# Four layers of cross-attention and FFN on one core: in the first FFN the rounding's constants move to ScalarE, the additions come one pair later, and the first products run three pairs ahead of the turned values

## The reference

```python
def fp4_quant_dequant(x):
    xb = x.reshape(shape[:-1] + (shape[-1] // 16, 16))
    scale = max(max(abs(xb)) / 6, 1e-12)
    xn = xb / scale
    idx = jnp.searchsorted(_MID, jnp.abs(xn))     # nearest of 0, .5, 1, 1.5, 2, 3, 4, 6
    return _GRID[idx] * jnp.sign(xn) * scale

h = silu(fp4_linear(x, w_gate)) * fp4_linear(x, w_up)   # 352 hidden values
x = x + tanh(g_ffn[0]) * fp4_linear(h, w_down)
```

## Time and profile before

| what | value |
|---|---|
| three runs | 792.27, 794.93, 795.2 us; median 794.93 |
| the profiled execution | 798.6 us, span from its first to its last instruction 796.8 us |
| mean granted TensorE clock | 0.897 |
| busy TensorE, VectorE, ScalarE, GpSimd | 629.9, 530.2, 325.5, 280.0 us |
| DMA | 67.73 MB, mean 85 GB/s |

### The profile page before, as it was taken

The page is one execution under the profiler, slowest core; times in us unless marked ns, Lnnn a source line. Parts: engine busy times, 40 slices in busy tenths (PEclk is TensorE's granted clock), DMA queues, the critical chain, the costliest instruction groups (busy, mean ns, idle before and its releaser), DMA issues.

```text
span 796.8 us, 10173 instructions
## 1 busy us (share of the span) xinstructions
PE 629.9 (79%) x3016; PEld 390.6 (49%) x3016; DVE 530.2 (67%) x1380; ACT 325.5 (41%) x627; POOL 280.0 (35%) x562
## 2 busy tenths in 40 slices
PE   4767876647899999898688771387887889999997
PEld 3433433334765564564334330143443666777885
DVE  8684646998762553378526647763558887998664
ACT  3142564223324334264153440315445455555553
POOL 5342354301240312115340721303123454546453
PEclk9795998777899999799899995579889999999999
DMA  8864421002204323002354330224400233444442
GB/s 260 185 172 129 86 59 55 2 0 67 66 24 135 94 42 89 8 17 77 106 147 145 58 79 0 66 70 109 136 5 1 81 90 104 119 103 110 117 120 67
DMA packets 67990, 67.73 MB, mean 85 GB/s; under 512 B 25119, under 2 KB 48223, under 8 KB 67552
## 3 DMA queue, kind: packets, MB, share of 16 engines
q1 hardware_dynamic: 61326, 64.61, 30.2%
q10 hardware_dynamic: 6610, 2.47, 1.3%
HBM read 50.29 MB, written 17.60 MB: 85 GB/s over the span
## 4 chain that ended last, share of the span: by engine, by line
PE 35%; DVE 22%; POOL 13%; issue 12%; DMA 9%; ACT 4%; SPq 4%; POOLq 0%; ACTq 0%; DVEq 0%
POOL sg L722 10%; PE ps L1803 7%; PE ps L1743 5%; PE ps L1783 5%; DVE mraw L1361 3%; DMA QG<-q_parts 3%; DMA q_parts<-loT 2%; PE ps L1705 2%; PE ps L1969 2%; SPq L330 2%; PE ps L1960 1%; PE ps L1722 1%; PE ps L1688 1%; PE ps L1694 1%; PE ps L1787 1%
## 5 line engine op out<-in xcount | busy, mean ns | idle before, releaser
L814 ACT ACTIVATE PT<-ps 110x512 f32<-110x512 f32 x192 | 111.0, 595 | 140.1 <-PE ps L1783 67.1
L1361 DVE TENSOR_REDUCE mraw<-ps 128x4 f32<-128x308 f32 x256 | 116.0, 475 | 76.8 <-PE ps L1743 31.5
L1743 PE MATMUL ps<-KG,QG 98*128 98x308 f32 x256 | 105.6, 430 | 46.3 <-DVE mraw L1361 25.8
L722 POOL TENSOR_TENSOR sg<-sg,cb 128x512 f32<-128x512 f32 x64 | 85.7, 1341 | 76.0 <-ACT sg L987 75.1
L1783 PE MATMUL ps<-QG,KG 128*110 128x512 f32 x192 | 90.9, 492 | 13.4 <-ACT PT L814 11.0
L1743 PEld LDWEIGHTS ps<-KG,QG 98*128 98x128 f32 x256 | 51.8, 206 | 89.4 <-DVE mraw L1361 60.6
L588 POOL TENSOR_TENSOR nt<-nhv,rs 128x4 f32<-128x4 f32 (+1 forms) x81 | 17.7, 218 | 165.8 <-DVE rs L1103 133.9
L1803 PE MATMUL ps<-PT,VN 128*18 128x512 f32 x512 | 72.2, 637 | 0.0
L1590 DVE TENSOR_TENSOR ps<-ps,sg 128x512 f32<-128x512 f32 x72 | 50.3, 698 | 32.3 <-POOL sg L722 29.3
L1783 PEld LDWEIGHTS ps<-QG,KG 128*110 128x110 f32 x192 | 33.9, 180 | 56.6 <-ACT PT L814 42.5
L987 ACT ACTIVATE sg<-ps 128x512 f32<-128x512 f32 x72 | 43.1, 599 | 42.6 <-PE ps L2031 42.2
(11 more groups left out here) (308 smaller groups left out, 1433.2 us busy)
## 6 DMA issues: line engine op xcount, KB each, us to landing
cb<-c_parts SPq DMA_DIRECT2D x64, 256.0 KB, 3.3
QG<-q_parts SPq DMA_DIRECT2D x48, 256.0 KB, 4.0
KG<-k_parts SPq DMA_DIRECT2D x48, 154.0 KB, 3.0
q_parts<-hiT SPq DMA_DIRECT2D x14, 256.0 KB, 2.0
q_parts<-loT SPq DMA_DIRECT2D x14, 256.0 KB, 2.0
k_parts<-kmH SPq DMA_DIRECT2D x16, 154.0 KB, 2.3
k_parts<-kmL SPq DMA_DIRECT2D x16, 154.0 KB, 2.8
VN<-v_parts SPq DMA_DIRECT2D x16, 144.0 KB, 2.8
```

Source lines behind the costliest of these rows:

```text
L722: pool.tensor_tensor(sg[:, n % 3, :], sg[:, n % 3, :], cb[:, k % CRING, :], ALU.mult).then_inc(sc_done, 1)
L814: act.activation(PT[0:w, q % PTR, :], ps[0:w, 4 + q % 2, :], ACT.Exp, scale=SCALE[l]).then_inc(exp_done, 1)
L1361: dve.tensor_reduce(mraw[:, n % 2, i, g * HG:(g + 1) * HG], ps[:, u % 2, 0:GK].rearrange("p (h k) -> p h k", k=K), AX_X, ALU.max).then_inc ...
L1743: ins = pe.matmul(o, QG[0:KS, n % 3, g, q], KG[0:KS, n % 3, g, :], start=True, stop=l not in (1, 2))
```

## The change

- VectorE's rounding is cut into `scaled(j)` (scales, product with the inverse scale, exponent bits) and `rounded(j)` (addition and subtraction). `scaled(j)` follows `product(j)`, `rounded(j-1)` follows `scaled(j)`.
- The constant (maximum with 1, times 1.5 * 2^22) is made by ScalarE in two linked instructions on 704 columns, `steps(j)`: a Relu with scale and bias, and an addition. Their biases lie in a new tile `magic`, set by two memsets.
- The factor 1 - 2^-22 on the inverse scale goes into the product as a scalar_tensor_tensor, here and in `quantise_batch`.
- `hscale` has three slots.
- TensorE: `turn(2j-6)` follows `up(2j)`, `turn(2j-5)` follows `up(2j+1)`, `down` of both behind, and only then the transposes of input 2 or 3 and of layer-1 inputs. The last four tiles' turns and downs stand between layer 1's score units 1 and 8.
- ScalarE's queue follows; `residual(0)` and `residual(1)` come after `product(4)` and `product(6)` instead of after pairs 3 and 5.

```diff
@@ -162,7 +162,8 @@
...
         qs2 = sb("qs2", [P, 2, 2, 32])
-        hscale = sb("hscale", [P, 2, 44])
+        hscale = sb("hscale", [P, 3, 44])
+        magic = sb("magic", [P, 2])
         am = sb("am", [P, 16])
@@ -279,6 +280,7 @@
...
         z_scales, z_scaled, z_steps = sem("z_scales"), sem("z_scaled"), sem("z_steps")
+        h_bits, h_steps = sem("h_bits"), sem("h_steps")
         am_w_part, am_w_ps, am_w_all = sem("am_w_part"), sem("am_w_ps"), sem("am_w_all")
@@ -640,7 +642,7 @@
...
                 pool.wait_ge(hq_scaled, j + 1)
-                pool.tensor_tensor(h, v, hscale[:, j % 2, :].unsqueeze(2).to_broadcast([P, 44, 16]),
+                pool.tensor_tensor(h, v, hscale[:, j % 3, :].unsqueeze(2).to_broadcast([P, 44, 16]),
                                    ALU.mult).then_inc(hq_done, 1)
@@ -856,6 +858,8 @@
...
                             silu(c // 3 + 1)
+                        if k == B and l == 0 and c == 6:
+                            steps(0)
                         if c == 5 and 1 <= k <= last:
@@ -886,29 +890,43 @@
...
+            def steps(j):
+
+                w = qh[:, j % 2, 1, :]
+                act.wait_ge(h_bits, j + 1)
+                act.activation(w, w, ACT.Relu, bias=magic[:, 0:1], scale=1.5 * 2.0 ** 22).then_inc(h_steps, 1)
+                act.wait_ge(h_steps, 2 * j + 1)
+                act.activation(w, w, ACT.Identity, bias=magic[:, 1:2]).then_inc(h_steps, 1)
+
             def ffn0(xT_one, q_one):
...
                 xqT_out(1)
-                for j in range(2, T // 2 + 2):
+                for j in range(2, T // 2):
+                    if j == 5:
+                        normalise_out((2, 0))
+                    for h in range(2):
+                        silu(2 * j + h)
+                        if j >= 3:
+                            hT_out(2 * j - 6 + h)
+                    if j == 7:
+                        normalise_out((2, 1))
                     if j in (3, 5):
...
                     if j in (5, 7):
-                        normalise_out((2, j // 2 - 2))
-                    if j < T // 2:
-                        silu(2 * j)
-                        silu(2 * j + 1)
+                        xT_one(j // 2 - 2)
+                    steps(j - 1)
+                    if j in (5, 7):
+                        q_one(j // 2 - 2)
                     if j == 3:
                         normalise_out((1, B - 1))
-                    if j in (5, 7):
-                        xT_one(j // 2 - 2)
-                    if j >= 2:
-                        hT_out(2 * j - 4)
-                        if j in (5, 7):
-                            q_one(j // 2 - 2)
-                        hT_out(2 * j - 3)
+                hT_out(T - 6)
+                hT_out(T - 5)
+                steps(T // 2 - 1)
+                for i in range(T - 4, T):
+                    hT_out(i)
                 normalise_out((2, 2))
@@ -1010,9 +1028,10 @@
...
+
             def quant_steps(w, src, inv):
-                link(dve.tensor_tensor(w[0], src, inv, ALU.mult))
+                link(dve.scalar_tensor_tensor(out=w[0], in0=src, scalar=1.0 - 2.0 ** -22, in1=inv, op0=ALU.mult, op1=ALU.mult))
                 link(dve.tensor_scalar(w[1].bitcast(I32), w[0].bitcast(I32), EXP_BITS, None, ALU.bitwise_and))
@@ -1142,7 +1161,8 @@
...
                 link(dve.tensor_reduce(s[0], v, AX_X, ALU.max, apply_absolute_value=True))
-                link(quant_scales(s[0], s[1]))
+                link(dve.tensor_scalar(s[0], s[0], 1.0 / 6.0, 1e-12, ALU.mult, ALU.max))
+                link(dve.reciprocal(s[1], s[0]))
                 link(quant_steps(w, v, s[1].unsqueeze(2).to_broadcast([P, 32, 16])))
@@ -1320,17 +1340,29 @@
...
                 dve.wait_ge(h_done, j + 1)
+                if j >= 3:
+                    dve.wait_ge(hq_done, j - 2)
+                link(dve.tensor_reduce(hscale[:, j % 3, :], h.rearrange("p t (n e) -> p (t n) e", e=16), AX_X, ALU.max,
+                                       apply_absolute_value=True))
+
+            def scaled(j):
+
+                v = fh[:, j % 3, :, :].rearrange("p t (n e) -> p (t n) e", e=16)
+                w = [qh[:, j % 2, i, :].rearrange("p (b e) -> p b e", e=16) for i in range(2)]
+                s = hscale[:, j % 3, :]
+                link(dve.tensor_scalar(s, s, 1.0 / 6.0, 1e-12, ALU.mult, ALU.max))
+                link(dve.reciprocal(qs[:, 1, :], s))
                 if j >= 2:
                     dve.wait_ge(hq_done, j - 1)
-                link(dve.tensor_reduce(hscale[:, j % 2, :], h.rearrange("p t (n e) -> p (t n) e", e=16), AX_X, ALU.max,
-                                       apply_absolute_value=True))
+                link(dve.scalar_tensor_tensor(out=w[0], in0=v, scalar=1.0 - 2.0 ** -22, in1=qs[:, 1, :].unsqueeze(2).to_broadcast([P, 44, 16]),
+                                              op0=ALU.mult, op1=ALU.mult))
+                dve.tensor_scalar(w[1].bitcast(I32), w[0].bitcast(I32), EXP_BITS, None, ALU.bitwise_and).then_inc(h_bits, 1)
             def rounded(j):
-
-                v = fh[:, j % 3, :, :].rearrange("p t (n e) -> p (t n) e", e=16)
-                w = [qh[:, j % 2, i, :].rearrange("p (b e) -> p b e", e=16) for i in range(2)]
-                link(quant_scales(hscale[:, j % 2, :], qs[:, 1, :]))
-                quant_steps(w, v, qs[:, 1, :].unsqueeze(2).to_broadcast([P, 44, 16])).then_inc(hq_scaled, 1)
+                w = [qh[:, j % 2, i, :] for i in range(2)]
+                dve.wait_ge(h_steps, 2 * j + 2)
+                link(dve.tensor_tensor(w[0], w[0], w[1], ALU.add))
+                dve.tensor_tensor(w[0], w[0], w[1], ALU.subtract).then_inc(hq_scaled, 1)
                 dve.wait_ge(hq_scaled, j + 1)
@@ -1401,8 +1433,10 @@
...
                     if c == 3 and l == 0 and k == B:
+                        link(dve.memset(magic[:, 0:1], -1.5 * 2.0 ** 22))
+                        link(dve.memset(magic[:, 1:2], 1.5 * 2.0 ** 22))
                         product(0)
-                        rounded(0)
+                        scaled(0)
                     if c == 9 and k == 0 and l == 0:
@@ -1475,17 +1509,18 @@
...
                     product(j)
+                    if j in (4, 6):
+                        residual(j // 2 - 2)
                     if j == 1:
...
                         quantise_batch(3)
-                    rounded(j)
-                    if j == 3:
-                        residual(0)
+                    scaled(j)
+                    rounded(j - 1)
                     if j == 5:
                         q_rest(0)
-                        residual(1)
                 q_rest(1)
+                rounded(T // 2 - 1)
                 for u in range(4 * TPB):
@@ -1923,29 +1958,42 @@
...
                 input_transposed(1)
-                for j in range(2, T // 2 + 2):
+                for j in range(2, T // 2):
+                    for h in range(2):
+                        up(2 * j + h)
+                        if j >= 3:
+                            turn(2 * j - 6 + h)
+                    if j >= 3:
+                        down(2 * j - 6)
+                        down(2 * j - 5)
                     if j in (3, 5):
                         input_transposed((j + 1) // 2)
-                    if j < T // 2:
-                        up(2 * j)
-                        up(2 * j + 1)
+                    if j == 5:
+                        pe.wait_ge(xqT_ready, B)
                     if j in (5, 7):
                         turn_input(j // 2 - 2)
-                    if j == T // 2 + 1:
-                        pe.wait_ge(silu_done, T)
-                        for u in range(2 * TPB):
-                            scores(0, u // G, u % G)
-                    if j >= 2:
-                        turn(2 * j - 4)
-                        if j >= 3:
-                            down(2 * j - 5)
-                        if j in (5, 7):
-                            queries(j // 2 - 2)
-                        turn(2 * j - 3)
-                        down(2 * j - 4)
-                down(T - 1)
-                for u in range(2 * TPB, 4 * TPB):
+                        queries(j // 2 - 2)
+                turn(T - 6)
+                turn(T - 5)
+                down(T - 6)
+                down(T - 5)
+
+                pe.wait_ge(silu_done, T)
+                for u in range(4 * TPB):
                     scores(0, u // G, u % G)
+                    if u == 1:
+                        turn(T - 4)
+                        turn(T - 3)
+                        down(T - 4)
+                    if u == 2:
+                        down(T - 3)
+                    if u == 4:
+                        turn(T - 2)
+                    if u == 6:
+                        turn(T - 1)
+                        down(T - 2)
+                    if u == 8:
+                        down(T - 1)
```

## The result

| | before | changed |
|---|---|---|
| median, first comparison (4 runs each) | 794.62 us | 784.15 us |
| ratio with its 95% interval | | 0.9864 [0.9838, 0.9891] |
| profiled execution, span | 798.6, 796.8 us | 782.29, 780.4 us |
| mean granted clock | 0.897 | 0.910 |

The change is worth 1.1 to 1.6%. Two later comparisons of the same kernel gave 0.9889 [0.9832, 0.9946] and 0.9867 [0.9843, 0.9892].

The account below looks back on a forecast made before the run. VectorE was taken to bound the kernel up to layer 1's first maxima, then TensorE's scores. VectorE's -8.4 and +3.1 made 5.3 us earlier; TensorE's scores left -5.0, so 794.93 - 5.0 = 789.9 us, range 786 to 797.

Parts of the forecast that it names:

- What VectorE saves: VectorE up to layer 1's first maxima: constant moved to ScalarE, factor folded, a wait and a slowed residual gone; -8.4 us.
- The -1.3 for product(5): VectorE's 1.28 us wait before product(5) goes, because the transposes of input 3 now stand behind pair 5's first products.
- What the new order adds: Four new VectorE waits, at batch 3's projection, product(3), rounded(2) and product(4): +1.0, +0.65, +0.3, +1.15, sum +3.1 us.
- Behind it TensorE decides: Layer 1's first scores: TensorE limits, score unit 2 comes only 3.8 us earlier; gain between 3.8 and near 8 us.
- I take a third of the way: -5.0: Score phase of layer 1: gain set a third of the way from 3.8 to near 8 us, so -5.0 us.
- B: Rival, layer 1's scores: all turns and downs disappear between scores and the clock rises early; -8, 787 us; chance 0.13.
- The rule against the change: Skill page keeps max, add, mul on VectorE; by it the move costs 9.9 us against 4.5 gained; not followed.
- the 4.5 booked: Gain booked for moving the maximum-and-scale from VectorE to ScalarE in the pairs: 8 x 0.56 = 4.5 us.
- C: Rival, inside the pairs: TensorE replaces VectorE as limit, bursts staying low; 4 us given back, 794 us; chance 0.26.
- D: Rival, layer 1's first 26 score units: clock stays low as turns and downs tear scores apart; +6, 801 us; chance 0.08.
- E: Rival, ScalarE in the pairs: Relu isn't in Silu's table, so each pair loads two tables; 795 us; chance 0.06.

## Why the prediction was wrong, point by point

- **What VectorE saves** held. L1017 and L1025 are gone at their sizes, the scalar_tensor_tensor costs 0 more (891 against 893 ns), no wait stands before product(5), and the residual of batch 3 takes 0.75 instead of 1.25 us. The -1.3 for product(5) rested on one profile: the wait was 1.28 us there and 0.60, 0.95 and 1.22 in three other executions. Missed: that contact with GpSimd wasn't removed but moved. The addition at 196.17 took 0.62 us more beside the multiplication from 195.55 to 196.94.
- **What the new order adds** held in sum, and in the first profile in place: 1.07 for 1.0 at the projection, 1.39 for 0.65 at product(3), 0.14 for 0.3 at rounded(2), 1.26 for 1.15 at product(4): 3.9 for 3.1. In the other two profiles it was 1.49 and 1.48 at the projection, 0.35 and 0.55 at product(3), 0.69 and 0.88 at product(4), and 1.02 and 1.13 at product(6), where the prediction saw 0.5 us to spare: 3.6 and 4.0 in all. Product starts relative to product(0) were 8.2, 19.1, 26.2, 33.4, 49.0, 55.4 and 65.7 us, laid out as 8.3, 19.3, 25.85, 33.2, 48.9, 55.4 and 65.9. With the slowed addition the first maximum came 74.6 behind, not 74.25; against the earlier trace rows that is 4.9 us earlier for 5.3, in the means 4.2. Part of the agreement is luck, for a gain was missing from the sum. The late addition doesn't depend on the operation ahead of it and starts 0.44 us behind that one's start; in the kernel before it did, and started 0.56 behind. First the changed kernel, then the kernel before:

```profile
140.86 0.53 DVE L1359 TENSOR_SCALAR qh<-qh 128x704 int32<-128x704 int32 x1
141.30 0.89 DVE L1364 TENSOR_TENSOR qh<-qh 128x704 f32<-128x704 f32 x1
```

```profile
205.47 0.53 DVE L1017 TENSOR_SCALAR qh<-qh 128x704 f32<-128x704 f32 x1
206.03 0.89 DVE L1018 TENSOR_TENSOR qh<-qh 128x704 f32<-128x704 f32 x1
```

Seven times 0.12 are 0.8 us. With the slowed addition, -8.4 - 0.8 + 3.9 + 0.6 = -4.7, near the -4.9 measured.
- **Behind it TensorE decides** is the step that failed, in "I take a third of the way: -5.0". Unit 2 did come as laid out, a little better: 199.62 - 124.02 = 75.6 behind product(0), against 80.03 in the kernel before, 4.4 earlier for 3.8. But from there to the end of the sixteenth maximum 3.2 more were won (14.4 before, 11.2 now), where of the 4.2 between "3.8" and "near 8" only 1.2 was booked. Two parts were undersized. The clock was to be up from unit 4 on; it was 0.50 up to about 197 us, in unit 0, and 1.00 from unit 2 through the whole stretch. Turns and a down now stand in the place of the pause of 2.49 us, and the longest pause left there is 0.72:

```profile
198.68 0.52 PE L1943 MATMUL ps<-ident,fh 128*128 128x128 f32 x3 [0.72 <-ACT hqT L905]
```

The clock held up is worth 0.8 to 1.9 us (idle matmuls in the old kernel). And turns and downs between scores cost almost no maximum its time: block against interleaving is 14.35 against 12.35 in the changed kernel, and 14.42 against 11.98 and 11.64 with the clock up in the old one, 2.0 to 2.8 us. Against rival B the prediction held TensorE's 7.2 busy us of 7.3. In the changed kernel it is just as busy (3.82 of 3.85 us, 3.79 of 3.90), but at full clock, with the turns and downs among the scores: a busy share at 0.54 of the clock was no argument.
- **The sum**: -4.2 and -3.2 make -7.4; with this the forecast would have been 787.5, next to B's 787 and inside the range. The measured 784.15 lies 3.4 us lower still. The prediction had everything ahead of product(0) at nothing; 2.0 to 2.8 us of difference stand there, for which no cause is shown and of which chance may be a part. Only with this did the time fall out of the range.
- **The rule against the change.** The Trainium skill, ScalarE: Activation LUTs, section Rules for kernel authors, would keep such operations on VectorE. Read as engine time the rows agree (0.53 us there, two of 0.88 here). Read as time of the kernel they don't: with the operation back on VectorE the first stretch is 0.9 to 1.7 us longer, though the timed runs can't tell the two apart. Of the 4.5 booked, 0.85 went into the wait at the projection, 0.53 at product(3), 1.26 at product(4) and 0.14 at rounded(2), which leaves 1.7. The 8.4 and the 3.1 are not separate worths.
- **Rivals.** B, with a chance of 0.13, is what the score phase did: turns and downs all but disappear, and the clock is up from the start of the stretch. C and D needed a low clock in the bursts or after 210 to cost time. Of C a part happened: pair 3's burst ran low (0.50) in all three profiles and pair 6's in two, where product(6) waited 1.02 and 1.13 us for the 1.0 of C; but the products waited 2.1 to 2.7 us in all, not C's 4.15. D did not: after 198.65 the clock was 1.00. E didn't happen: sixteen steps between Silus, no load; the same page's section Table sets: the hidden batching unit had said so, and here the trace agrees.

## What to carry to other kernels

A row that shows TensorE busy all the time at half clock says little of what fits in there at full clock: ask first what pauses stand ahead of the fall, and whether work that waits behind the stretch can fill them. Before moving an operation from the short engine to an idle one with three times its duration in all (0.53 us against two of 0.88), see that what wants the result comes later than the slower engine needs: the one-pair distance made it a small gain here, 0.9 to 1.7 us in the traces, and the same move without it lost 18.5 us. Price such a move by putting it back alone, since waits take up most of what the row promises.

## What was not expected of the hardware

VectorE and GpSimd held each other up, but only in some pairings. GpSimd's rows around the addition of 1.51 us, and four-column operations beside VectorE's additions and products:

```profile
144.55 0.20 POOL L590 TENSOR_TENSOR nt<-nhv,rs 128x4 f32<-128x4 f32 x1
...
145.70 0.93 POOL L590 TENSOR_TENSOR nt<-nhv,rs 128x4 f32<-128x4 f32 x1
146.71 0.48 POOL L591 TENSOR_TENSOR nt<-nt,rs 128x4 f32<-128x4 f32 x1
...
195.55 1.39 POOL L645 TENSOR_TENSOR fh<-qh,hscale 128x704 f32<-128x704 f32 x1 [4.36 <-DVE qh L1365]
```

The same operation on the same four columns took 0.20 us beside VectorE's maxima and 0.93 beside its product of `fh` with the inverse scales, two tiles in SBUF (L1357, 145.69 to 146.58). Product(2) and its block maxima (143.15, 144.08), beside a multiplication from 143.20, took their usual 0.89: one reads PSUM, the other a single tile. The addition at 196.17 ended 0.74 us behind the multiplication, the tensor_scalar at 153.04 only 0.04 behind. The Trainium skill, SBUF — State Buffer, section Who interferes with whom, gives this as a port that whoever starts first keeps for its whole instruction, with a TENSOR_TENSOR from two SBUF tiles and some tensor_scalars among the takers and reductions not; the rows agree. Three such contacts cost VectorE 0.5 (before), 0.62 and 1.1 us. They depend on tenths of a microsecond, so a kernel whose waits are shortened can lose part of it there, as the one with 34 idle matmuls did.

TensorE's clock doesn't follow from the length of the last pause. It was low again behind pauses of 2.49 us (before, 209.07), 3.02 (22 idle matmuls) and 8.29 (changed kernel, 144.19), still high behind 0.66 and 0.98. But it was also high behind 2.63, in the changed kernel's pair 2 (two matmuls in 0.83 us, where they take 1.51 at the low clock), and in the second profile of the kernel before it fell ahead of 212.90, with no pause over 1.15 us since TensorE's last low burst. From the changed kernel:

```profile
133.29 0.83 PE L1932 MATMUL ps<-wqt,xnT 128*128 128x352 f32 x2 [2.63 <-DVE fh L1341]
...
144.19 1.51 PE L1932 MATMUL ps<-wqt,xnT 128*128 128x352 f32 x2 [8.29 <-DVE fh L1341]
```
